# A decoder of eight gated blocks on one core: the state-space block's second half prepared during the first half's rounds, and the first attention head's keys made alone

## The reference

```python
# block 1, state space (16 states; per channel e, batch b, time t; B, C, dt from one projection of u)
u = silu(causal_conv4(in_proj_w @ ctx) + conv_b)
delta = softplus(dt_proj_w @ dt_lo + dt_proj_b);  A = -exp(A_log)
state = state * exp(delta * A) + (delta * u) * B;  y = sum_n(state * C) + D * u
x = x + tanh(g) * y * silu(layernorm(x))
# block 2, quantised feed forward
x = x + tanh(g) * qlinear(silu(qlinear(n, w_gate)) * qlinear(n, w_up), w_down)
# block 3, cross attention, 16 heads of 128, q and k each divided by its root mean square
x = x + tanh(g) * (softmax(q @ k.T / sqrt(128)) @ v) @ Wo
```

## Time and profile before

| | us |
|---|---|
| median of 3 runs (lowest, highest) | 1015.46 (1014.79, 1017.61) |
| time of the profiled execution | 1015.46 |
| its span in the trace | 1012.7 |
| TensorE busy in the span | 911.6 |
| DVE busy | 718.1 |
| ACT busy | 646.1 |
| POOL busy | 484.5 |

### The profile page before, as it was taken

One profiled execution on the slowest core, in us unless ns is written; L12 is line 12 of the kernel. 1 busy time (PEld: TensorE's weight loads), 2 busy tenths in 40 slices (PEclk: granted clock), 3 DMA queues, 4 the chain that ended last, 5 costly groups with the idle time before them and its releaser, 6 DMA issues.

```text
span 1012.7 us, 15673 instructions
## 1 busy us (share of the span) xinstructions
PE 911.6 (90%) x5322; PEld 747.7 (74%) x5322; DVE 718.1 (71%) x1301; ACT 646.1 (64%) x1252; POOL 484.5 (48%) x480
## 2 busy tenths in 40 slices
PE   5367677677999999999989999999999999999998
PEld 1022223346899999999977888888888888888887
DVE  7799998995777777777657675786665655666554
ACT  5857764685777777777665676656667644554553
POOL 0166653034676666666444343454344544344342
PEclk8589979797899999999999999999999999999999
DMA  9300100002100000000008611221112500021121
GB/s 289 157 0 1 62 2 0 1 1 99 60 1 1 2 1 2 1 2 1 2 33 305 216 54 52 58 65 56 43 53 63 230 1 2 1 74 53 60 65 44
DMA packets 17466, 55.97 MB, mean 55 GB/s; under 512 B 3057, under 2 KB 4185, under 8 KB 15245
## 3 DMA queue, kind: packets, MB, share of 16 engines
q1 hardware_dynamic: 5197, 34.01, 9.2%
q10 hardware_dynamic: 12192, 20.98, 6.9%
HBM read 53.82 MB, written 1.16 MB: 54 GB/s over the span
## 4 chain that ended last, share of the span: by engine, by line
PE 51%; DVE 12%; POOL 7%; issue 7%; ACT 4%; ACTq 1%; DMA 1%; DVEq 0%; POOLq 0%
PE psum L431 15%; PE psum L433 14%; PE psum L432 14%; POOL a_P L1963 3%; DVE a_max L1676 2%; POOL a_rk L1890 2%; POOL a_rq L1898 2%; DVE psum L1607 1%; PE psum L825 1%; DVE psum L1809 1%; PE psum L749 1%; PE psum L683 1%; PE psum L785 1%; DVE bn_st L1293 1%; ACT L1110 1%
## 5 line engine op out<-in xcount | busy, mean ns | idle before, releaser
L431 PE MATMUL psum<-x_norm_T_hi,f_wgu_hi 128*128 128x512 f32 x400 | 160.3, 401 | 3.0 <-DVE f_h_lo L1816 3.0
L433 PE MATMUL psum<-x_norm_T_hi,f_wgu_lo 128*128 128x512 f32 x400 | 157.5, 394 | 0.0
L432 PE MATMUL psum<-x_norm_T_lo,f_wgu_hi 128*128 128x512 f32 x400 | 156.8, 392 | 0.0
L431 PE MATMUL psum<-f_wd_hi,f_h_hi 128*128 128x256 f32 x400 | 121.8, 304 | 0.1
L1607 DVE TENSOR_TENSOR psum<-f_silu,psum 128x512 f32<-128x512 f32 x100 | 69.3, 693 | 69.6 <-PE psum L433 46.8
L433 PE MATMUL psum<-f_wd_hi,f_h_lo 128*128 128x256 f32 x400 | 112.9, 282 | 0.0
L432 PE MATMUL psum<-f_wd_lo,f_h_hi 128*128 128x256 f32 x400 | 112.9, 282 | 0.0
L1984 POOL TENSOR_TENSOR m_dBu<-m_du,m_Bs 128x1024 f32<-128x1024 f32 x32 | 76.3, 2384 | 68.5 <-DVE m_du L1405 24.8
L1816 DVE TENSOR_TENSOR f_h_lo<-psum,f_h_hi 128x512 fp32r<-128x512 f32 x100 | 68.9, 689 | 51.7 <-ACT f_h_hi L871 51.1
L1903 POOL TENSOR_TENSOR f_wgu_lo<-f_w,f_wgu_hi 128x512 fp32r<-128x512 f32 x44 | 56.8, 1292 | 93.9 <-ACT f_wgu_hi L871 93.9
L1903 POOL TENSOR_TENSOR f_wgu_lo<-f_wb,f_wgu_hi 128x512 fp32r<-128x512 f32 x36 | 46.6, 1295 | 103.2 <-ACT f_wgu_hi L871 103.2
(11 more groups left out here) (317 smaller groups left out, 2630.9 us busy)
## 6 DMA issues: line engine op xcount, KB each, us to landing
f_cw<-r_rows ACTq DMA_DIRECT2D x38, 256.0 KB, 3.2
f_wb<-in_f1b SPq DMA_DIRECT2D x6, 1152.0 KB, 8.9
f_w<-in_f3w SPq DMA_DIRECT2D x1, 5376.0 KB, 16.3
f_wa<-in_f1a SPq DMA_DIRECT2D x1, 3840.0 KB, 11.8
w_raw<-in_w0raw SPq DMA_DIRECT2D x1, 3072.0 KB, 18.9
f_w<-in_f2w SPq DMA_DIRECT2D x2, 1536.0 KB, 9.4
f_cw<-r_rows ACTq DMA_DIRECT2D x12, 224.0 KB, 3.0
f_cw<-r_rows ACTq DMA_DIRECT2D x12, 192.0 KB, 2.9
```

The costliest lines, as they stand in the source:

```text
L431: mm(out, wh, xh, start=start, stop=False, **kw)
L432: mm(out, wh, xl, start=False, stop=False, **kw)
L433: return mm(out, wl, xh, start=False, stop=stop, **kw)
```

## The change

- The convolution of (half 1, group 0) moves from DVE to TensorE: four matmuls with shifted inputs, each with one tap folded into the input weights. The 256 KB `taps` are loaded for it behind `small`, ahead of `x`, and POOL folds them. ACT then reads PSUM.
- D * u is added by two matmuls with diagonal weights (`direct(h)`) in front of a half's identity matmuls, which POOL prepares; `gated(h)` keeps one of its two steps.
- ACT loses max(v,0) and the bf16 copy of B and C; DVE takes them (`positive_part`, first line of `split`).
- `delta` is done on DVE for half 0 alone, group by group, and round 0's POOL product too. For half 1 POOL does its three steps behind the products of rounds 3, 6 and 9, and ACT's inverse stands in round 0. The absolute sums move to rounds 1, 2 and 3.
- In tile 7 statistics and the rounding of tile 6 come ahead of `q_h`. POOL raises head 0's four columns first; DVE scales head 0's keys alone, then tile 7's scale, and the other heads' keys in two parts. The first key transpose uses bank 5; `last_hidden_T` comes after `scores(0)`, `last_down` follows the next keys; POOL's context remainder follows the first query norm.
- In pass 30 the low part of the probabilities comes ahead of `keys_lo(31)`, and in passes 30 and 31 the reciprocal comes ahead of the router's steps.

The core of the diff (indentation cut by four):

```diff
+INV = [dA[0], spl]
...
+    ("ctxT", ctxT, 0, "ctx"), ("m_in", m_in, 0, "ctx"), ("small", small, 0, "small"), ("taps", tapw, 0, "taps"),
...
-        for h in range(2):
-            for e in range(2):
...
+        for h, e in ((0, 0), (0, 1), (1, 1)):
+            mm(ps[:, 4 * h + e, :], m_in[:, e * P:(e + 1) * P], ctxT[:, h * HALF:(h + 1) * HALF],
+               start=True, stop=True).then_inc(S("m_x"), 1)
+        pe.wait_ge(S("m_prepared"), 1)
+        dst, src = (a.rearrange("p (b l) -> p b l", b=2) for a in (ps[:, 4, :], ctxT[:, HALF:2 * HALF]))
+        for s_ in range(4):
+            last = mm(dst[:, :, s_:DM], tapw[:, 3 - s_, :], src[:, :, 0:DM - s_], start=s_ == 0, stop=s_ == 3,
+                      skip_group_check=True)
+        last.then_inc(S("m_x"), 1)
...
+        def direct(h):
+            pe.wait_ge(S("m_prepared"), 2)
+            for e in range(2):
+                mm(ps[:, e, :], diagD[:, e, :], u[h][:, e, :], start=True, stop=False)
...
+        direct(0)
...
+                    pe.wait_ge(S("m_yz"), 1)
+                    direct(1)
...
+                if i == 1:
+                    pe.wait_ge(S("a_ktok"), 3)
...
+            pe.wait_ge(S("a_ktok"), min(i + 1, KB) + 2 if i else 1)
...
+            else:
+                pe.wait_ge(S("a_ktok"), 2)
...
+        last_hidden_T()
...
+                last_down()
...
+            if (h, e) == (1, 0):
+                act.wait_ge(S("m_x"), 4)
...
+            A(u[h][:, e, :], ps[:, 4, :] if (h, e) == (1, 0) else dlt[h][:, e, :], ACT.Silu, bias=small[:, c_cb + e:c_cb + e + 1]).then_inc(S("m_u"), 1)
...
-            copy(bcs[h][:, :], ps[0:96, 2 + 4 * h, :]).then_inc(S("m_p1"), 1)
...
-                b_ = small[:, c_dtb + e:c_dtb + e + 1]
-                A(y[:, e, :], ps[:, 4 * h + e, :], ACT.Abs, bias=b_).then_inc(S("m_abs"), 1)
-                last = A(dlt[h][:, e, :], ps[:, 4 * h + e, :], ACT.Relu, bias=b_)
-            last.then_inc(S("m_xs"), 1)
+                A(y[:, e, :], ps[:, 4 * h + e, :], ACT.Abs, bias=small[:, c_dtb + e:c_dtb + e + 1]).then_inc(S("m_abs"), 1)
...
-            A(y[:, :, :], lnw[:, :, :], ACT.Exp, scale=-1.0).then_inc(S("m_inv"), 1)
+            A(INV[h][:, :, :], SOFTPLUS[h][2][:, :, :], ACT.Exp, scale=-1.0).then_inc(S("m_inv"), 1)
...
+        inverse(0)
...
+            if g == NS:
+                act.wait_ge(S("m_du"), 3)
...
+                if g == 0:
+                    act.wait_ge(S("m_du"), e + 1)
...
-                for i in range(3):
-                    last = link(sum_weights(i)) if i < 2 else sum_weights(i)
-                last.then_inc(S("wabs_part"), 1)
+                inverse(1)
+            if g in (1, 2):
+                link(sum_weights(g - 1))
+            if g == 3:
+                sum_weights(2).then_inc(S("wabs_part"), 1)
...
+        squares(0)
+        keys_hi(0)
+        last_hidden_round()
...
+        last_hidden_copy()
...
+            link(V.tensor_copy(bcs[h][:, :], ps[0:96, 2 + 4 * h, :]))
...
+        def positive_part(h):
+            dve.wait_ge(S("m_abs"), 2 * h + 2)
+            for e in range(2):
+                last = V.tensor_scalar(dlt[h][:, e, :], ps[:, 4 * h + e, :], small[:, c_dtb + e:c_dtb + e + 1], 0.0, ALU.add, ALU.max)
+            last.then_inc(S("m_xs"), 1)
...
-            link(V.tensor_tensor(dlt[h][:, :, :], dlt[h][:, :, :], lnw[:, :, :], ALU.add))
...
-            link(V.tensor_tensor(du[h][:, :, :], du[h][:, :, :], inv[:, :, :], ALU.mult))
-            link(V.tensor_tensor(dlt[h][:, :, :], dlt[h][:, :, :], du[h][:, :, :], ALU.subtract))
-            V.tensor_tensor(du[h][:, :, :], dlt[h][:, :, :], u[h][:, :, :], ALU.mult).then_inc(S("m_du"), 1)
+            V.tensor_tensor(dlt[h][:, :, :], dlt[h][:, :, :], lnw[:, :, :], ALU.add).then_inc(S("m_rem"), 1)
...
+        def delta(e):
...
+            dve.wait_ge(S("m_inv"), 1)
+            dve.wait_ge(S("m_rem"), 3)
+            link(V.tensor_tensor(du[0][:, e, :], du[0][:, e, :], INV[0][:, e, :], ALU.mult))
+            link(V.tensor_tensor(dlt[0][:, e, :], dlt[0][:, e, :], du[0][:, e, :], ALU.subtract))
+            V.tensor_tensor(du[0][:, e, :], dlt[0][:, e, :], u[0][:, e, :], ALU.mult).then_inc(S("m_du"), 1)
...
-        conv(1, 0)
+        row_stats(1, 0, TH)
...
-        stats(1)
+        variance()
...
+        positive_part(0)
...
+        positive_part(1)
...
-            for e in range(2):
-                last = V.scalar_tensor_tensor(dlt[h][:, e, :], u[h][:, e, :], small[:, c_D + e:c_D + e + 1], ps[:, e, :], ALU.mult, ALU.add)
-            last.then_inc(S("m_y_read"), 1)
-            dve.wait_ge(S("m_y_read"), h + 1)
...
+                if g:
+                    dve.wait_ge(S("m_dBu"), g + 2)
...
+                    if g == 0:
+                        dve.wait_ge(S("m_dBu"), e + 1)
...
+            if t == NT - 1:
+                dve.wait_ge(S("q_out"), TH)
+                stats(0)
+                within_8_bits(NT - 2)
...
-                dve.wait_ge(S("q_out"), TH)
-                stats(0)
-                within_8_bits(NT - 2)
+                normalise(0, xn[0])
...
+                first_head_scaled()
...
+    def first_head_scaled():
+        dve.wait_ge(S("a_rk"), 1)
+        for n, bank in enumerate(KEY_BANKS):
+            last = V.tensor_scalar(ktok[0][:, n, 0, :], ps[:, bank, 0:P], rk0[:, 4 * n:4 * n + 1], None, ALU.mult)
+        last.then_inc(S("a_ktok"), 1)
...
+    def other_heads_scaled(*units):
...
+        dve.wait_ge(S("a_rk"), 2)
+        for n in units:
+            last = V.tensor_tensor(ktok[0][:, n, 1:4, :], ps[:, KEY_BANKS[n], P:4 * P].rearrange("p (n d) -> p n d", n=3),
+                                   bc(rk0[:, 4 * n + 1:4 * n + 4].unsqueeze(2), [P, 3, P]), ALU.mult)
+        last.then_inc(S("a_ktok"), 1)
...
+        other_heads_scaled(1, 2)
...
+        other_heads_scaled(0, 3)
...
+                else:
+                    keys_lo(i + 1)
...
+            if i == HEADS2 - 2:
+                keys_lo(i + 1)
...
+            dve.wait_ge(S("a_exp"), i + 1)
+            if i:
+                dve.wait_ge(S("a_pn"), i)
+            V.reciprocal(ri[:, :], rs[:, :]).then_inc(S("a_ri"), 1)
...
+        if i == 0:
+            by_head = rk0[:, :].rearrange("p (n c) -> p n c", c=4)
+            for heads in (slice(0, 1), slice(1, 4)):
+                G.tensor_tensor(by_head[:, :, heads], by_head[:, :, heads], bc(mhalf[:, :].unsqueeze(2), [P, TH, heads.stop - heads.start]),
+                                ALU.pow).then_inc(S("a_rk"), 1)
...
+    loaded(pool, "m_in", "taps")
+    G.tensor_tensor(tapw[:, :, :], tapw[:, :, :], bc(m_in[:, 0:P].unsqueeze(1), [P, 4, P]), ALU.mult).then_inc(S("m_prepared"), 1)
...
+    loaded(pool, "ident", "small")
+    for e in range(2):
+        last = G.tensor_scalar(diagD[:, e, :], ident[:, :], small[:, c_D + e:c_D + e + 1], None, ALU.mult)
+    last.then_inc(S("m_prepared"), 1)
...
+            pool.wait_ge(S("a_ctkh"), 1)
+            G.tensor_tensor(ctkl[:, :, :], ctk[:, :, :], ctkh[:, :, :].bitcast(f32), ALU.subtract).then_inc(S("a_ctk"), 1)
...
+            def delta1(step):
+                pool.wait_ge(S("m_inv"), 2)
+                pool.wait_ge(S("m_rem"), 4)
+                pool.wait_ge(S("m_prepared"), 2 + step)
+                if step == 0:
+                    G.tensor_tensor(du[1][:, :, :], du[1][:, :, :], INV[1][:, :, :], ALU.mult).then_inc(S("m_prepared"), 1)
+                if step == 1:
+                    G.tensor_tensor(dlt[1][:, :, :], dlt[1][:, :, :], du[1][:, :, :], ALU.subtract).then_inc(S("m_prepared"), 1)
+                if step == 2:
+                    G.tensor_tensor(du[1][:, :, :], dlt[1][:, :, :], u[1][:, :, :], ALU.mult).then_inc(S("m_du"), 1)
...
+            for e in range(2):
+                pool.wait_ge(S("m_Bcopy"), 1)
+                pool.wait_ge(S("m_du"), e + 1)
+                G.tensor_tensor(dBu[0][:, e, :], du[0][:, e, :], Bs[0][:, :], ALU.mult).then_inc(S("m_dBu"), 1)
+            for g in range(1, 2 * NS):
...
+                pool.wait_ge(S("m_du"), 3 if g >= NS else 2)
...
+                if g in (3, 6, 9):
+                    delta1(g // 3 - 1)
```

More of the change, by code:

```diff
@@ L482, in ssm @@
                     if g == NS + 1:
-                        pe.wait_ge(S("m_y_read"), 1)
+                        pe.wait_ge(S("m_yz"), 1)
+                        direct(1)
                     for e in range(2):
-                        last = mm(ps[:, e, :], ident[:, :], hC[(g - 1) % 2][:, e, :], start=(g - 1) % NS == 0, stop=(g - 1) % NS == NS - 1)
+                        last = mm(ps[:, e, :], ident[:, :], hC[(g - 1) % 2][:, e, :], start=False, stop=(g - 1) % NS == NS - 1)
                     last.then_inc(S("m_y"), 1)
@@ L715, in attn1 @@
                 if i == 0:
-                    last_hidden_T()
+                    last_down()
                 if i >= 2:
@@ L753, in attn1 @@
                     keys_T(i + 1)
-                if i == 0:
-                    last_down()
                 if i == 2:
```

(17 more changed lines are left out.)

75 lines of the change are left out of this document (22 added, 53 removed).

## The result

Changed kernel: 1005.28 us, median of 4 runs (1004.32 to 1006.18), against 1015.61 (1014.79 to 1017.61) for the kernel before: ratio 0.9897, 95% interval 0.9884 to 0.9909. A later set of 4 runs gave 1004.79 and 0.9903 (0.989 to 0.9917). "Lead" is how much earlier an instruction starts than its like in the kernel before. The spans don't hold the whole gain. All eight executions of the changed kernel had 1.8 us of their time outside the span, the 62 of the kernel before that the runs list 1.8 to 3.1, 2.6 in the mean. So some 0.8 of the 10.3 us lies where no trace looks.

A forecast was written before the change was run, and what follows sets the result against it. DVE bounds the rounds, TensorE the heads from 262 us, and chains through all engines the preparation and attention start. Terms 2.4 + 3.8 - 1.2 - 1.2 + 0.2 + 0.8 + 1.3 = 6.1 off 1015.46 gave 1009.4 us, range 1005.5 to 1014.

The forecast's parts named there:

- Preparation: Chain up to the first `delta(0)`, old start 39.55 us: 2.4 us earlier (0.8 to 3.5).
- the projection ends at 16.1 instead of 16.7: TensorE's second projection in the preparation: waits for `m_dtw` until 14.4 us, then four instructions take 1.65 instead of 3.30.
- The 1.0 us for the taps' load: Start of the preparation: 256 KB of taps ahead of `x` and `m_dtw` delay these loads by 1.0 us.
- Delta to round 0: From `delta(0)` to the end of round 0's scans at 45.0 us (old 51.2): 3.8 us gained, 6.2 earlier in all.
- Rounds 1 to 4: DVE's scans wait for exponents behind ACT's sums; round 5 starts at 61.9 instead of 66.94 us, 5.0 earlier.
- Between the halves: Gate to round 19: eight TensorE instructions stall it 2.3 us, DVE saves 1.40; 1.2 us given back with a small echo.
- End of `M`: At the second gate a saving of 1.4 us ends at ACT's table load before `q_h`: 0.2 us gained.
- Handover: Quantised stage to first head: first normalised probabilities 0.8 us earlier than 248.63 (bounds -1.2 and +2.0).
- Last heads: TensorE's 1.75 us wait for the probabilities' low part goes by swapping it with `keys_lo(31)`: 1.3 us gained.
- In pass 31 the router's end moves only 0.2: Router's steps in pass 31, last heads: their end moves only 0.2 us and is not what is late.
- rivals: Handover gives nothing, 0.23; head start mostly given back or POOL steps push products past scans, 0.19; TensorE bounds early rounds, 0.04.
- The case that I gave 0.04: A greater gain: clock kept at the gate and handover at its upper bound, 1005.5 us; chance 0.04.

The follow-up runs named there:

- e3: Kernel before with only the last heads' order of the change (passes 30 and 31): 1015.31 us, ratio 0.9998.
- e7: Kernel before with six idle transposes of the identity on TensorE in pass 1 of the heads: 1010.70 us, ratio 0.9966.
- e8: Kernel before with the taps loaded ahead of x and not used: 1015.21 us, ratio 0.9999.
- e14: Changed kernel with the convolution of half 1, group 0 on DVE again, taps still loaded and multiplied: 1008.12 us, ratio 0.9933.
- e2: Kernel before with only the handover part (tile 7's order, first head's keys alone, pass 0): 1013.13 us, ratio 0.9977.
- e4: The whole change without its handover part, against the kernel before: 1006.29 us, ratio 0.9909.
- e15: The changed kernel run once more, unchanged: 1004.79 us, ratio 0.9903.
- e1: Kernel before with only the state-space part (preparation, tap matmuls, D on TensorE, halves' delta, sums in rounds 1 to 3): 1007.27 us, ratio 0.9918.
- e5: Changed kernel with the router's DVE steps ahead of the reciprocals and its exponents ahead of the head's again: 1003.12 us, ratio 0.9888.

## Why the forecast was wrong, point by point

- **Preparation** (2.4 forecast, 3.4 measured). The step "the projection ends at 16.1 instead of 16.7" failed. I read TensorE's wait for `m_dtw` and the four instructions of 3.30 us as part of the chain; e3, e7 and e8 have the same code, the copy of dt 1.6 to 2.0 us earlier, and the steps behind within 0.2 of where they were. The chain there is DVE's convolutions (e14: 3.06 us). In e3 and e8 TensorE has no such wait, in e7 it ends 1.2 us earlier. The price per microsecond was wrong too: in the changed kernel dt's copy came 1.4 us ahead of the forecast, but ACT then needed 11.0 us to the end of the exponent where I had 10.2 (12.8 less 2.4 less 0.4 is 10.0 in fact), so only 0.5 was left of it; DVE's queue behind it and the steps after that give the other 0.5. The 1.0 us for the taps' load did not show in e8 or in the changed kernel, where `m_dtw` was there in time. e2 shows what it costs when it isn't: 1.8 us. The copy from PSUM cost 0.68, as priced.
- **Delta to round 0** (3.8 forecast, 3.9 measured, a lead of 7.3). Steps of 512 columns took 0.69, the exclusion came once, POOL's three steps cost nothing: right.
- **Rounds 1 to 4** ("0 in round 2, 0.7 in round 3, 0.5 in round 4"). The waits were 0.72 and 0.26, at TensorE's mean clock of 0.64 in 20 to 60 us where it had been 0.50, and 1.08 for POOL where 1.2 was forecast. My own terms also add up to 61.6 (46.2, four rounds of 3.54, 1.2 of waits) and not to 61.9. Lead 6.8, in the mean of six profiles 6.7 by the 16th product (108.34 for the old code, 101.64 for the new), instead of 5.0.
- **Between the halves** ("2.3 us stall, less 1.4 saved"). The 1.4 is right. The stall is close to 2.3 (2.13 to 2.25) in half of the six profiles and 0.55 in the rest. What failed is that I priced it against one profile of before as if its rounds 16 to 31 were fixed, and put the new stall on top of the 1.76 us that stood there already: 4.4 us of waits with the echo, where the new rounds have 2.1 in the mean and the old ones 1.7. The rounds take 63.9 to 67.3 us for the same code, mean 65.8, and 64.8 in the mean of the six new ones. So 1.0 is gained there where I gave back 1.2: a miss of 2.2. Whether the new order also moves the waits behind the gate, six profiles against five don't settle.
- **End of `M`**: the last product at 174.14 and 166.42 in the means, a lead of 7.7 against 3.8 forecast (2.4 + 3.8 - 1.2 - 1.2). That is a surplus of 3.9 us: 1.0 from the preparation, 0.7 from rounds 1 to 4, 2.2 from rounds 16 to 31. Behind `M` the span gains 1.7 more (9.4 in the mean of eight executions) where 2.3 were forecast, and the 0.8 us outside the span, for which I had no term, bring the sum to 4.1 of the 4.2.
- **Handover** (0.8 forecast, 1.0 measured by e4): right in sum by two errors. In the first profile the chain itself lost 0.6 from the end of `M` to the probabilities (in e15 0.1), because the squares' lead fell to 6.8 on the late fourth key unit, 1.6 below that at the end of `M`, where I had priced 0.6; the head's scaling took 1.12, as priced. Then head 2 gave 1.7, its low stretch being absent, in all ten profiles with this part. e7 gains the same 1.7 there without the part, so this stretch of low clock is what it is.
- **Last heads** (1.3 forecast, 1.0 by e1 against e4 and rough, nothing by e3, 0 to 0.5 in the traces). The wait fell by 1.2 as worked out. "In pass 31 the router's end moves only 0.2" was wrong: the reciprocal ahead of it lets POOL's product in, and e5 shows 1.7 us in this.

Of the rivals, none came true. The case that I gave 0.04, the clock kept at the gate and the handover at its upper bound, has the time but not the reason: e15's profiled execution had the whole stall at the gate and still took 1005.71, and the handover gave half of its bound. The kept clock is rather a term than a case, since in some executions it is kept and in some not. So my theory of the surplus holds for its place, the state-space part (e1). The clock as its reason is shown for the size of the stall at the gate and not for the rest.
